# One early dense product instead of two, and the second layer's dense products behind the second list

## The reference, cut to what matters

```python
x = x + xattn(layernorm(x), ctx, ctx, mask, Wq..bo)     # 16 heads, 64 keys
x = x + ffn(layernorm(x), P_w, U1, U2, U3, W1, W2, b2)
# ffn, with f = layernorm(x) as 2048 rows of 256:
#   a = f @ P_w.T ; C1, C2, C3 = top-3 softmax of a @ U1.T, a @ U2.T, a @ U3.T over 12 experts
#   h = gelu(sum_e C1[:, e] * (f @ W1[e].T))
#   y = sum_e C2[:, e] * (h @ W2[e].T) + C3 @ b2
```

## Time and profile before

| | us |
|---|---|
| median of 3 runs | 356.67 (356.38 to 358.89) |
| the profiled execution | 361.34 |
| its span, first to last instruction | 359.6 |
| PE busy | 326.2 (91%) |
| POOL busy | 231.1 (64%) |

### The profile page before, as it was taken

The page is one execution under the profiler, slowest core; times in us unless marked ns, Lnnn a source line. Parts: engine busy times, 40 slices in busy tenths (PEclk is TensorE's granted clock), DMA queues, the critical chain, the costliest instruction groups (busy, mean ns, idle before and its releaser), DMA issues.

```text
span 359.6 us, 7758 instructions
## 1 busy us (share of the span) xinstructions
PE 326.2 (91%) x2089; PEld 284.9 (79%) x2089; DVE 251.2 (70%) x842; ACT 199.2 (55%) x485; POOL 231.1 (64%) x329
## 2 busy tenths in 40 slices
PE   3889999999899897978999999898998999999995
PEld 3678997898798776956999888676787888898883
DVE  3798977889678977387698635277778545454596
ACT  2295897998567673252777551333315777782000
POOL 4457487767667675610777877577753777777484
PEclk9998998999699999699999999999999999999999
DMA  7910022221221127440577826553226767641596
GB/s 212 356 72 4 1 63 78 95 93 60 62 103 49 46 96 237 151 124 0 168 225 216 269 86 203 207 155 146 108 101 195 233 205 223 204 163 37 165 389 207
DMA packets 33889, 52.21 MB, mean 145 GB/s; under 512 B 6090, under 2 KB 23860, under 8 KB 33720
## 3 DMA queue, kind: packets, MB, share of 16 engines
q1 hardware_dynamic: 26472, 35.35, 31.7%
q0 software_dynamic: 6816, 16.24, 12.5%
q10 hardware_dynamic: 560, 0.13, 0.2%
HBM read 29.75 MB, written 24.82 MB: 152 GB/s over the span
## 4 chain that ended last, share of the span: by engine, by line
PE 55%; DVE 15%; issue 11%; POOL 7%; ACT 7%; DMA 4%; DVEq 0%; SPq 0%; ACTq 0%; POOLq 0%
PE banks L1685 30%; PE banks L1774 4%; PE banks L1970 3%; PE banks L1756 2%; PE banks L1731 2%; POOL list_rows L726 2%; DMA y_token<-prob_t,bo_sb 2%; PE banks L1741 2%; POOL w_l L597 2%; DVE xf_t L1290 2%; PE banks L1744 2%; PE banks L1746 2%; DVE q_hl L1081 2%; DMA y_token<-prob,bo_sb 1%; PE banks L1817 1%
## 5 line engine op out<-in xcount | busy, mean ns | idle before, releaser
L1685 PE MATMUL banks<-w_h,xd 128*128 128x512 f32 x288 | 93.0, 404 | 3.1 <-DVE xn_t L1290 2.0
L1685 PE MATMUL banks<-w_h,bt 128*128 x328 | 69.3, 304 | 2.2 <-DVE bt L1459 2.0
L1685 PEld LDWEIGHTS banks<-w_h,xd 128*128 128x128 f32 x288 | 53.7, 191 | 16.0 <-DVE xn_t L1290 1.7
L700 POOL DMA_INDIRECT y_token<-prob,bo_sb x42 | 41.2, 981 | 35.0 <-DVE bo_sb L1461 25.9
L1685 PE MATMUL banks<-w_l,xd 128*128 128x512 f32 x144 | 57.5, 399 | 0.0
L1685 PEld LDWEIGHTS banks<-w_h,bt 128*128 128x128 f32 x328 | 49.7, 189 | 5.1 <-issue 3.8
L700 POOL DMA_INDIRECT y_token<-prob_t,bo_sb x40 | 39.2, 981 | 12.6 <-issue 6.0
L1685 PE MATMUL banks<-w_l,bt 128*128 x164 | 46.1, 281 | 0.0
L1459 DVE TENSOR_TENSOR bt<-banks,bt 128x256 fp32r<-128x256 f32 x82 | 34.0, 416 | 10.7 <-ACT bt L938 10.4
L1290 DVE SCALAR_TENSOR_TENSOR xf_t<-banks,mask_all,xf_t 128x256 f32<-128x256 f32 x60 | 25.1, 477 | 22.6 <-ACT xf_t L848 20.4
L938 ACT ACTIVATE bt<-banks 128x256 fp32r<-128x256 f32 x82 | 31.1, 380 | 12.3 <-PE banks L1970 11.3
(11 more groups left out here) (236 smaller groups left out, 758.6 us busy)
## 6 DMA issues: line engine op xcount, KB each, us to landing
late_rows<-list_rows SPq DMA_DIRECT2D x62, 136.0 KB
stage<-in_w_t_dram SPq DMA_DIRECT2D x12, 512.0 KB, 3.7
list_rows<-wo_sb SPq DMA_DIRECT2D x26, 136.0 KB, 1.8
stage<-y_token SPq DMA_DIRECT2D x8, 384.0 KB
late_rows<-y_token SPq DMA_DIRECT2D x6, 384.0 KB, 3.8
mid<-y_token SPq DMA_DIRECT2D x6, 384.0 KB, 5.2
out_dram<-x_all SPq DMA_DIRECT2D x16, 128.0 KB, 2.5
wq_sb<-list_rows SPq DMA_DIRECT2D x10, 136.0 KB
```

The lines of the kernel that those rows point to most:

```text
L700: pool.indirect_dma_start(out=y_token[i][:, :], out_offset=bass.IndirectOffsetOnAxis(block_at[:, g:g + 1], 0), in_=y_out[g % OUTS], in_off ...
L1685: ins = pe.matmul(dst, a(c), b(c), start=(i == 0), stop=(i == len(terms) - 1))
```

## The change

- `EARLY_SLOTS` goes from 2 to 1 and `MID` from 9 to 8. Slot 1 (tile 9) is now between the lists, slot 8 (tile 12 of layer 2) behind the second list. PE's order becomes: attention with slot 0; first list; slots 1 to 7; second list; slots 8 to 11.
- In the attention's last iterations four of slot 0's pairs are done in iterations 14 and 15, one in 16 and one behind; the transpose of the places (`transpose_table(0)`) moves behind `logits(12)` and a pair, and `logits(12)` no longer waits for the table; on DVE `table_as_rows(0)` moves behind `xd_low(12)`; `transpose_xf(13)` moves to the front of iteration 16.
- The low parts of weight pairs 9, 10 and 11 move from DVE to POOL, between its last normalisation steps and in front of the first `send_block`.
- Between the lists the orders of ACT and DVE are written anew; the gelu, transpose and rounding of tile 15 move into the second list's first blocks.
- PE loads the second list's weight places in front of slot 7 and not behind all products.
- `PE_TAILS` loses tile 2, which POOL adds up instead.

```diff
-    PE_TAILS = (2, 6, 10)
+    PE_TAILS = (6, 10)
-    EARLY_SLOTS, MID = 2, 9
+    EARLY_SLOTS, MID = 1, 8
+            def split_late(n):
+                pool.wait_ge(w_hi, n + 1)
+                pool.wait_ge(w_split_late, n - EARLY)
+                pool.tensor_tensor(w_l[:, n, :, :], stage[:, n % RING, :, :], w_h[:, n, :, :].bitcast(F32),
+                                   ALU.subtract).then_inc(w_split_late, 1)
...
+                if t == 16:
+                    split_late(EARLY + 1)
+            split_late(EARLY + 2)
+            split_late(EARLY + 3)
...
@@ ACT
-            first_pair(1)
             copy_xf(14)
...
-            first_pair(2)
+            first_pair(1)
             gelu_rows(8)
             gelu_rows(9)
+            first_pair(2)
             gelu_rows(10)
             first_pair(3)
...
-            gelu(15)
-            first_pair(8)
-            h_high(15)
...
+                if j == 0:
+                    gelu(T - 1)
+                if j == 3:
+                    h_high(T - 1)
@@ DVE
-                    split_low(EARLY + 1)
-                    xd_low(13)
-                    split_low(EARLY + 2)
-            sum_pairs(1, range(1, 3))
             xd_low(14)
-            split_low(CHUNKS - 1)
-            sum_pairs(1, range(3, PAIRS))
...
+            sum_pairs(1, range(1, PAIRS))
             sum_pairs(2, range(1, PAIRS))
-            sum_pairs(3, range(1, PAIRS))
             sum_rows(0)
+            sum_pairs(3, range(1, 3))
             sum_rows(1)
...
@@ PE
                 if t == 15:
-                    pe.wait_ge(table, TABLE)
                     logits(12)
                     early_pairs(2, 3)
+                    transpose_table(0)
+                    early_pairs(3, 4)
...
-            early_pairs(5, 8)
-            transpose_xf(14)
...
             load_weight_places(0)
-            early_pairs(8, 2 * PAIRS)
+            early_pairs(5, PAIRS)
+            transpose_xf(14)
             transpose_block(0, 0)
...
+                if slot == MID - 1:
+                    pe.wait_ge(table, 2 * TABLE)
+                    load_weight_places(1)
                 expert_pairs(slot, range(0, 4))
                 transpose_h(S1 + slot - 1)
                 expert_pairs(slot, range(4, PAIRS))
-            pe.wait_ge(table, 2 * TABLE)
-            load_weight_places(1)
...
             pe.wait_ge(h_lo, T - S)
+            expert_pairs(8, range(PAIRS))
             expert_pairs(9, range(PAIRS))
             expert_pairs(10, range(PAIRS))
             add_rows(0)
-            expert_pairs(11, range(0, 3))
+            expert_pairs(11, range(0, 5))
             add_rows(1)
-            expert_pairs(11, range(3, 5))
-            add_rows(2)
             expert_pairs(11, range(5, PAIRS))
```

More of the change, by code:

```diff
@@ L1400, in _ @@
                     xd_low(t - 3)
+                if t == 15:
+                    table_as_rows(0)
                 if t == 9:
@@ L1461, in block_low @@
                 dve.tensor_copy(block_at[:, g:g + 1], block_in[g % LOADS][:, AT:AT + 1].bitcast(I32)).then_inc(at_kept, 1)
-            finds = ((1, 0, 0, 4), (1, 4, 4, 4), (1, 8, 8, 4), (0, S1 + 2, DENSE_AT, 2), (0, S, DENSE_AT + 2, 4),
-                     (1, S, DENSE_AT + 6, 4)) + tuple((2, t, BIAS_AT + t, 4) for t in range(0, T, 4))
+            finds = ((1, 0, 0, 4), (1, 4, 4, 4), (1, 8, 8, 4), (0, S1 + 1, DENSE_AT, 3), (0, S, DENSE_AT + 3, 4),
+                     (1, S, DENSE_AT + 7, 4)) + tuple((2, t, BIAS_AT + t, 4) for t in range(0, T, 4))
             found = {slot: i + 1 for i, (_, _, slot, _) in enumerate(finds)}
@@ L1614, in _ @@
                     dense_route(j - 26)
+            sum_pairs(1, range(1, PAIRS))
             sum_pairs(2, range(1, PAIRS))
-            sum_pairs(3, range(1, PAIRS))
             sum_rows(0)
+            sum_pairs(3, range(1, 3))
             sum_rows(1)
-            sum_pairs(4, range(1, 3))
-            sum_pairs(4, range(3, 5))
+            sum_pairs(3, range(3, PAIRS))
             sum_rows(2)
-            sum_pairs(4, range(5, PAIRS))
+            sum_pairs(4, range(1, 4))
             sum_rows(3)
-            sum_pairs(5, range(1, 3))
+            sum_pairs(4, range(4, PAIRS))
+            sum_pairs(5, range(1, 4))
             h_low(12)
-            sum_pairs(5, range(3, 4))
             sum_rows(4)
             sum_pairs(5, range(4, PAIRS))
+            sum_pairs(6, range(1, 3))
             sum_rows(5)
-            sum_pairs(6, range(1, 3))
+            sum_pairs(6, range(3, 4))
             h_low(13)
-            sum_pairs(6, range(3, 4))
             sum_rows(6)
             sum_pairs(6, range(4, PAIRS))
+            sum_pairs(7, range(1, 3))
             sum_rows(7)
-            sum_pairs(7, range(1, 3))
+            sum_pairs(7, range(3, 4))
             h_low(14)
[L1639 to L1645, removed]
+            sum_pairs(7, range(4, PAIRS))
             for j in range(BLOCKS[1]):
-                if j > 0:
-                    block_low(FIRST[1] + j)
+                block_low(FIRST[1] + j)
+                if j == 4:
+                    h_low(T - 1)
                 if j < 7:
@@ L1655, in _ @@
                     add_bias(C3_AT.index(j - 3))
-            sum_pairs(9, range(1, PAIRS))
-            sum_pairs(10, range(1, 3))
+            sum_pairs(8, range(1, PAIRS))
+            sum_pairs(9, range(1, 5))
             sum_tail(0)
-            sum_pairs(10, range(3, 4))
             sum_tail(1)
-            sum_pairs(10, range(4, PAIRS))
[L1663 to L1668, removed]
+            sum_pairs(9, range(5, PAIRS))
+            sum_tail(2)
+            for pair in range(1, 4):
+                sum_pairs(10, (pair,))
+                sum_tail(2 + pair)
+            sum_pairs(10, range(4, PAIRS))
             sum_tail(6)
             sum_tail(7)
-            sum_pairs(11, range(3, 4))
+            sum_pairs(11, range(1, 2))
             sum_tail(8)
+            sum_pairs(11, range(2, 4))
+            sum_tail(9)
             sum_pairs(11, range(4, 5))
-            for t in range(9, S):
-                sum_tail(t)
+            sum_tail(10)
+            sum_tail(11)
             sum_pairs(11, range(5, PAIRS))
@@ L1907, in _ @@
                     transpose_probs(t)
-                if t == 15:
-                    transpose_table(0)
+                if t == 16:
+                    transpose_xf(13)
                 transpose_a(t - 1)
@@ L2099, in _ @@
                 multiply_block(1, j)
+                if j == 2:
+                    transpose_h(T - 1)
                 if j - 2 in C3_AT:
```

25 lines of the change are left out of this document (9 added, 16 removed).

## The result

The changed kernel takes a median of 361.01 us (358.15 to 364.85, 20 runs) where the kernel before takes 359.02 (356.14 to 362.44, 20 runs beside them): a ratio of 1.0062, 95% interval 1.0035 to 1.0089. I had forecast a gain of 4.3; it lost about 2.2, and 1 lies outside the interval. The median lies outside the range of 350.3 to 358.0.

The account below looks back on a forecast made before the run. From the first send on, POOL's lists and row sends with SP's issue form one serial chain; PE sets the end. Profiled, -12.1 + 8.44 - 1.29 = -4.9 us; with a gain of 4.3 taken, the median is 352.4, range 350.3 to 358.0.

Parts of the forecast that it names:

- The first send: Start of the first list: POOL's three low parts bound it, at 159.6 us, 12.1 earlier than 171.66.
- The tail: Behind the second list: PE runs 36.4 us without idle, with one product more and one group of adding matmuls less.
- The lock between DVE and POOL: At the front: slot 0's last DVE add may wait for a POOL low part, first send about 0.5 later.
- the sum: Whole kernel: -12.1 at the first send, +8.44 and -1.29 behind the second list, making -4.9 us.
- POOL's row sends, the DMA wait in them and SP's issue keep their distance from the first send: Between the lists: these stages keep their lengths, so SP issues the second list at 256.2 and transposes start at 258.5.
- rival C: Row sends between the lists wait for slot 1; one product late, 8.44, makes it 3.5 slower, 360.2; chance 0.11.
- its threshold of 4.9: Added waiting in the row sends, in us, from which the slower outcome decides.
- signs of being wrong: First send later than 164.5, a wait for the gelu rows in the row sends, or half clock at either list's start.
- Rival B: Clock falls at PE's new waits: 2.1 at the second list, about 1.0 at the first; 354.6 to 358; chance 0.20.
- the 3.7: PE's forecast wait in us ahead of the second list, from 254.8 to transposes at 258.5.
- B's own condition: PE idles about 3 us before the first block and 3.7 before the second list, and the clock falls.
- The clock's 2.7: Front, 144 to 152: 2.7 of up to 3.4 us lost to low clock; the gain is 2.2 if timed runs lacked it.

Follow-up runs that it names:

- e1: Changed kernel with DVE's row sums of tiles 5 and 7 put ahead of two pairs' sums; ratio 0.9963 to the kernel before.
- e7: Changed kernel with 18 unused matmuls on PE at the first list's start; ratio 1.0052 to the kernel before.
- e10: Changed kernel with slot 0's last add on DVE moved behind the seventh block's low part; ratio 1.0005 to the kernel before.
- e3: Changed kernel with slot 8 back between the lists and the old order behind the second list; ratio 0.9876 to the kernel before.
- e5: Kernel before's front, with only slot 8 moved behind the second list; ratio 1.0288 to the kernel before.
- e2: Changed kernel with 24 unused matmuls in PE's wait ahead of the second list; ratio 1.0004 to the kernel before.
- e9: e3 with 18 unused matmuls on PE at the first list's start; ratio 0.9842 to the kernel before.
- e4: e3 and e1 together; ratio 0.9909 to the kernel before.
- e6: Changed kernel with the low parts of weight pairs 9, 10 and 11 back on DVE; ratio 1.0117 to the kernel before.
- e11: e3 with e7's matmuls, e1's earlier sums and e10's later add; 352.83 against 359.32 us, ratio 0.9819.

## Why the prediction was wrong

**Right.** The first send came behind three POOL low parts of 2.4, bound by POOL and the first block's path as laid out. That it came at 158.99 against 159.6 is luck: the mark was 1.89 earlier than in the execution that I worked from. The tail was 36.47 without idle against 36.4. The second list's wait on PE ends 2.4 after SP's issue, as before. The lock between DVE and POOL was seen too; I priced it at 0.5 and left it out of the sum, and it was 1.0.

**The step that failed** is "POOL's row sends, the DMA wait in them and SP's issue keep their distance from the first send". They did not: the row sends alone took 2.9 more. I laid the gelus out against PE's products and found 2 to 5 us of slack for the later tiles. The row sum on DVE that each gelu needs was not in that layout, and it stands in order behind sums of the next product. With one product less ahead of the sends, and with the sums of tiles 5 and 7 moved behind other sums by the change itself, this order gave POOL the two waits, 2.53 and 0.97, that e1 takes away by going back to the old order. It is kin to rival C, which also had the new orders hold up the row sends: not at slot 1's tile but at tiles 5 and 7, a third of the price of 8.44, and well under its threshold of 4.9. Two of my signs of being wrong came up: a wait for the gelu rows among the sends, and the clock at half at a list's start.

**Rival B, given 0.20, was right too.** The sum put the clock's price at nothing at both lists. It was at 0.50 at the second list's start and 0.60 at the first's. That cost about 1.2 to 1.3 of list 1 (e7, e10), where I had 1.0. At the second list I had 2.1: the changed kernel's profile paid 1.3 (0.9 on the first block, 0.4 on the rest), the other five profiles with the low clock there 1.7 to 2.5. The wait was 6.63, not 3.7, because the 3.7 was worked from the same fixed distances; but e1, with 3.58, had the fall as well, so B's own condition was enough. With B's 2.9 of the missed 7.1, it weighed as much as the row sends. The Trainium skill, TensorE: Matmul & The Clock Gate, section Why this matters for your kernels, asks for no idle gaps between bursts; by that rule B had to come, and the rows at the second list agree.

**Mis-sized.** Mark to first send: 12.19 where I had 10.9. e10 gives back 1.0 of the 1.3: DVE's add waited for POOL's low part, and the first block's `bt` stood behind it.

**What this did to the sum.** The second list had to come more than 7.15 earlier to pay for the product behind it. I let it come 12.1 earlier; PE's transposes came 6.25 earlier (115.63 against 121.88). And by my own numbers the change was not the best use of its front: with PE waiting 3.7 there, slot 8 in that place would have reached 4.7 past it, less than the 7.15 that it costs behind the list. e3 and e5 separate the halves: the front gains 3.4 by the profile and 4.4 by the ratio, and slot 8's move costs 5.6 with the new front (6.7 by the ratios) and, by the ratio, 10 with the old. The start of the second list is set by the later of two arrivals, POOL's rows and PE's last product, and a product taken from PE there brings only what PE had been late by.

**The clock's 2.7 and the base.** I took 2.7 as a part of the fall that would or would not carry over. As a size it was good: e5 without the fall is 2.45 quicker from the mark to the first send. Without it before's PE's end would lie near 204.0 (an estimate, 206.44 - 2.45), and the change would lose about 4.7 and not 2.2 in the profile; the timed 2.2 is nearer to the table as it stands, and how often before's timed executions had the fall isn't shown. The mark itself lay anywhere from 143.35 to 149.08 in these profiled executions, a spread of 5.7 that has nothing to do with the lists. It goes with the clock ahead of the mark. Added up over windows of 2 us, the falls there took away 1.7 us of full speed in e2 and e9 (marks 143.63 and 143.35), 3.4 in e3 (145.41), 5.1 in the changed kernel, e4, e5 and e10 (146.67 to 146.82) and 6.8 in before, e1, e6, e7 and e11 (148.40 to 149.08). Three runs were a poor base beside it.

**Open.** In which stages the timed executions of e5, and those of before, lost what their mean clocks show; why the clock fell early in the attention in some executions and not in others; why the start of the second list cost 1.3 to 2.5 at the same low clock.

## What to carry to other kernels

Where two engines meet at a seam, lay out both arrivals before moving work off one of them: moved work pays only up to the other arrival, and costs in full where it lands. For each transfer whose issue is to come earlier, follow its data back through every in-order queue, the small sums on DVE too, and not only through the engine with the large work. Where a change rewrites an engine's order, compare the place of each small item with the old order: going back for two sums here moved the ratio from 1.0062 to 0.9963. Then ask what the new wait does to PE's clock, and bound that by whichever engine paces the blocks.

## What the runs showed of the hardware

A DVE add of two SBUF tiles, 0.42 alone, took up to 2.19 beside a POOL instruction of 2.4. After 6.63 us without a matmul the granted clock was 0.50 in the 4 us in which the list began, and after 3.58 us (e1) too. With unused matmuls in most of that wait it was 1.00, and the first block's way from transpose to send took 3.70 instead of 4.62. Half speed for a few blocks cost 1.2 to 1.3 us at either list of the changed kernel, and up to 2.5 at the second list in other profiles. In the changed kernel and e1 that is less than the 3.4 us of full speed that the clock took away there, since POOL's send every 1.3 us sets the pace. In twelve profiles the mark came later the more the low clock had taken away ahead of it, from 143.35 with 1.7 us of full speed lost to 149.08 with 6.8.
